# One decoder layer with a mixture of experts: the up layer's bias moved from a TensorE product to a VectorE add

## The chip, the cores and the metric

The kernel runs on one core of a Trainium2 chip. The metric is device time in microseconds (us) of the whole program, the median of several runs. A profiled execution has a time of its own; its span runs from the first to the last instruction.

## The reference

One post-norm decoder layer over 2048 tokens of width 256, in float32: self-attention, a cross-attention that reduces to two weight products, and a feed-forward part with 8 experts of which each token uses two, beside a shared expert.

```python
x = layernorm(x + self_attention(x))
x = layernorm(x + cross_attention(x, context))
scores = softmax(x @ gate_w.T); topk_w, topk_i = top_k(scores, 2)          # weights rescaled to sum to 1
h  = silu(einsum('nd,edh->neh', x, up_w) + up_b)                           # up_b: one row of 256 per expert
ye = einsum('neh,ehd->ned', h, down_w) + down_b
x = layernorm(x + einsum('ned,ne->nd', ye, comb) + shared_expert(x))
```

## The kernel before

All products run in TensorE with both operands split in two float32r parts (`hi` and the rest `lo`); `three` (L307) issues hi x hi, hi x lo and lo x hi. Engines are programmed one by one and meet at semaphores; the order on each engine is written out by hand.

*Before the loop.* Attention runs in 34 slots (`all_slots`, L338). The gate's choice gives each token two places in `xg_dram`, a buffer sorted by expert, and GpSimd scatters the rows there (`send`, L597). VectorE makes lists of tiles of 128 rows: `list_early` (L1712) those of tiles 0 to 16, in slot 33, and `list_later` (L1741) the other 22, inside the loop. `list_e` holds each tile's expert (8 for a tile that isn't used), `list_row` its first row. `rows` (128 x 10 x 256) holds the bias rows of all experts, split, on a few partitions; `sel` is a matrix of ones and zeros that adds those partitions up, so that the product of `sel` and one expert's rows puts a bias on all 128 partitions.

*The expert loop.* TILES = 39 tiles, on each engine one loop over i:

- TensorE (L1090): `tile_up(i)` (the bias product L1028, then six products in `three`), `tile_turn_x(i + 2)` (two transposes, L1018), `tile_turn_h(i - 1)` (L1042), `tile_down(i - 2)` (bias product L1050, six products). At i in LOADS (0, 4, 8, 12, 16, 17, 21, ...) it first loads up to four expert numbers from `list_e` into registers (L1096), and the weights are addressed by these. `PIECES_AT` adds products of the shared expert after turns 8 and 10.
- ScalarE (L1397): `tile_silu(i)` (L1319), `tile_x_hi(i + 2)` (L1312), `tile_h_hi(i - 1)` (L1325), `tile_y(i - 2)` (L1332). After turn 8 it takes an exponential (L1336) for the gate's weights, which changes its table, and silu changes it back.
- VectorE (L1975): `tile_x_lo(i + 2)` (L1829), a share of the small work (`drip`: one or two operations of `list_later`, `weigh`, later `add_experts(0)`), `tile_h_lo(i - 1)` (L1834), more small work. From turn 36 on the small work is `add_experts(0)`, which begins with a wait for rows fetched by SyncE.
- SyncE (L438): the load of tile i (L452) once the x rest of tile i - 4 is done. Then it waits until the results of tiles 0 to 30 have landed, fetches the expert rows of the first three quarters of the tokens (`load_y`, L454, L457), and those of the last quarter after tile 38.
- GpSimd (L710): `target_of(i + 8)` (L627), which needs the load of tile i + 8, then `send_y(i)` (L633), which scatters tile i's result to `y_dram`.

A turn is one value of i. The x rest and the h rest are what L1829 and L1834 write. Two tiles are in flight in `t_up` (PSUM) and `th` (SBUF), by i % 2.

*After the loop* VectorE adds the two weighted expert rows of each token (L1885), takes moments (L1895) and the last norm; TensorE does so for one quarter of the tokens and half of another (L1113).

## Time and profile before

| | before |
|---|---|
| median of 3 runs, us (lowest, highest) | 461.9 (460.45, 462.31) |
| the profiled execution, us | 463.2 |
| its span, us | 461.5 |
| mean granted TensorE clock, share of full | 0.987 |
| busy: TensorE, VectorE, ScalarE, GpSimd, us | 439.5, 309.3, 297.4, 211.4 |

Views of the profile are used as follows. The chain that ended last follows the last instruction back to what released it, step by step; its shares say which engine sets the time. The windows give each engine's busy time in a stretch. The timeline lists instructions by start. Busy time of an engine that others wait for counts; that of one that waits for others doesn't. TensorE's products overlap: their pace is the distance between starts, not their length.

### The profile page before, as it was taken

What the parts mean: (1) busy time and instruction counts of PE and PEld (TensorE: products, weight loads), DVE (VectorE), ACT (ScalarE), POOL (GpSimd) and SP (SyncE); (2) the same over time, 40 slices, a digit from 0 to 9 for tenths busy, and PEclk for the clock granted to TensorE, in tenths of its full rate; (3) what the DMA queues carried; (4) which work ended last, traced back from release to release, by engine and by line L of the source; (5) the groups of instructions that cost most, each with busy time, mean ns of one, the idle gap of its engine ahead of it and who ended that gap; (6) DMA issues with size and microseconds to landing.
All of it is one profiled execution on the core that took longest, in us unless ns stands there. A gap on an engine that the chain in (4) does not pass through costs nothing.

```text
span 461.5 us, 11060 instructions
## 1 busy us (share of the span) xinstructions
PE 439.5 (95%) x3657; PEld 396.7 (86%) x3657; DVE 309.3 (67%) x1249; ACT 297.4 (64%) x922; POOL 211.4 (46%) x246
## 2 busy tenths in 40 slices
PE   7999999999999999999999999989988999999991
PEld 6889898988989889898898998978778999999971
DVE  4366676878786757598676869698886734333495
ACT  3688656676666865668667567765523686776535
POOL 1899498440205011211166454473344686566521
PEclk9999999999999999999999999998998999999997
DMA  5950121400300000020021223021023654443576
GB/s 155 313 187 0 62 92 47 139 0 1 132 8 1 1 24 24 25 70 0 1 60 53 78 76 104 1 71 48 23 69 95 178 176 130 127 125 118 192 267 205
DMA packets 26543, 40.16 MB, mean 87 GB/s; under 512 B 3199, under 2 KB 17683, under 8 KB 26483
## 3 DMA queue, kind: packets, MB, share of 16 engines
q1 hardware_dynamic: 21532, 27.86, 19.7%
q0 software_dynamic: 3408, 9.33, 5.6%
q10 hardware_dynamic: 1547, 2.27, 1.6%
q8 instruction: 31, 0.51, 0.5%
q14 instruction: 25, 0.20, 0.2%
HBM read 26.83 MB, written 12.61 MB: 85 GB/s over the span
## 4 chain that ended last, share of the span: by engine, by line
PE 79%; DVE 9%; DMA 3%; issue 3%; ACT 2%; POOL 2%; SPq 1%; ACTq 0%; POOLq 0%; DVEq 0%
PE bank L309 17%; PE bank L310 17%; PE bank L311 17%; PE bank L825 7%; PE bank L836 7%; PE bank L875 6%; DMA w_raw<-y_dram 2%; PE bank L1018 2%; PE bank L776 1%; PE bank L920 1%; PE bank L1042 1%; POOL y_dram L633 1%; DMA xacc<-in_x_t 1%; DVE xacc L1885 1%; PE bank L1028 1%
## 5 line engine op out<-in xcount | busy, mean ns | idle before, releaser
L1201 ACT ACTIVATE probs<-probs,negmax 128x128 f32<-128x128 f32 x256 | 99.7, 393 | 26.5 <-DVE negmax L1470 26.5
L1470 DVE CUSTOM_DVE_ANT_0 probs<-bank,mask 128x128 f32<-128x128 f32 x256 | 62.4, 285 | 46.2 <-PE bank L825 46.2
L309 PE MATMUL bank<-w_hi,ot_hi 128*128 (+1 forms) x284 | 81.4, 287 | 3.5 <-DVE ot_lo L1496 3.5
L310 PE MATMUL bank<-w_lo,ot_hi 128*128 (+1 forms) x284 | 81.1, 286 | 0.0
L311 PE MATMUL bank<-w_hi,ot_lo 128*128 (+1 forms) x284 | 80.9, 285 | 0.0
L309 PE MATMUL bank<-xt_hi,w_hi 128*128 128x512 f32 (+1 forms) x148 | 59.7, 403 | 0.7 <-DVE xt_lo L1439 0.4
L1481 DVE TENSOR_TENSOR probs<-probs,rsum 128x512 f32<-128x512 f32 x64 | 58.6, 916 | 2.2
L309 PEld LDWEIGHTS bank<-w_hi,ot_hi 128*128 128x128 f32 x284 | 54.9, 193 | 4.1 <-issue 4.1
L610 POOL DMA_INDIRECT xg_dram<-xacc,place x32 | 34.0, 1062 | 53.0 <-PE bank L836 29.6
L310 PE MATMUL bank<-xt_lo,w_hi 128*128 128x512 f32 (+1 forms) x148 | 57.6, 389 | 0.0
L311 PE MATMUL bank<-xt_hi,w_lo 128*128 128x512 f32 (+1 forms) x148 | 57.6, 389 | 0.0
L311 PEld LDWEIGHTS bank<-w_hi,ot_lo 128*128 128x128 f32 x284 | 54.9, 193 | 0.0
L310 PEld LDWEIGHTS bank<-w_lo,ot_hi 128*128 128x128 f32 x284 | 54.7, 192 | 0.0
L1213 ACT ACTIVATE ot_hi<-bank,cols 128x512 fp32r<-128x512 f32 x32 | 22.0, 686 | 49.8 <-PE bank L875 49.8
L1164 ACT ACTIVATE qkv<-bank,cols 128x512 f32<-128x512 f32 x64 | 43.8, 684 | 10.9 <-PE bank L311 10.7
L1201 ACT ACTIVATION_READ_ACCUMULATOR probs<-probs,negmax 128x1 f32 x256 | 48.7, 190 | 0.0
L1829 DVE TENSOR_TENSOR ot_lo<-bank,ot_hi 128x256 fp32r<-128x256 f32 x39 | 16.5, 424 | 46.5 <-ACT ot_hi L1312 46.3
L633 POOL DMA_INDIRECT y_dram<-qkv,w_raw x39 | 40.6, 1041 | 14.3 <-ACT qkv L1332 8.4
L309 PE MATMUL bank<-w_hi,xt_hi 128*128 128x256 f32 x160 | 46.8, 292 | 0.0
L310 PE MATMUL bank<-w_lo,xt_hi 128*128 128x256 f32 x160 | 44.8, 280 | 0.0
L311 PE MATMUL bank<-w_hi,xt_lo 128*128 128x256 f32 x160 | 44.8, 280 | 0.0
L825 PE MATMUL bank<-qkv 64*128 64x128 f32 x512 | 37.2, 285 | 0.0
(237 smaller groups left out, 1059.5 us busy)
## 6 DMA issues: line engine op xcount, KB each, us to landing
qkv<-xg_dram SPq DMA_DIRECT2D x39, 128.5 KB, 2.4
ex_raw<-in_w_experts SPq DMA_DIRECT2D x18, 256.0 KB, 2.7
w_raw<-in_w_quads SPq DMA_DIRECT2D x10, 256.0 KB, 4.6
xacc<-in_x SPq DMA_DIRECT2D x4, 512.0 KB, 4.3
ex_raw<-in_w_cross SPq DMA_DIRECT2D x4, 512.0 KB, 3.8
w_raw<-in_ctx_t_in ACTq DMA_DIRECT2D x4, 512.0 KB, 3.8
w_raw<-in_w_quads SPq DMA_DIRECT2D x3, 512.0 KB, 6.5
xacc<-in_x_t SPq DMA_DIRECT2D x3, 512.0 KB, 6.8
```

What stands on the lines that cost most here:

```text
L309: pe.matmul(o, a_hi, b_hi, start=first, stop=False)
L310: pe.matmul(o, a_hi, b_lo, start=False, stop=False)
L311: return pe.matmul(o, a_lo, b_hi, start=False, stop=last)
L610: pool.indirect_dma_start(xg_dram, bass.IndirectOffsetOnAxis(ap=place[:, g, i, j:j + 1], axis=0), xacc[:, g * GT + j, :], None).then_inc(s ...
L633: pool.indirect_dma_start(y_dram, bass.IndirectOffsetOnAxis(ap=target[:, i:i + 1], axis=0), yt[:, i % YR, :], None).then_inc(y_sent[i % YR ...
L825: mm = pe.matmul(sc_bank[h][:, slices(j, P)], qt[s.ub][rows_h, s.pp, slices(j, P)], kt[s.ub][rows_h, s.pp, slices(j, P)], start=True, stop ...
L836: mm = pe.transpose(tr_bank[h][:, slices(j, P)], probs[:, 1 - s.par, h, slices(j, P)], ident[:, :])
L875: mm = pe.matmul(pv_bank[slices(h, DH), slices(j, P)], vb[:, j, c:c + DH], probs_t[:, h, slices(j, P)], start=True, stop=True)
L1164: nc.scalar.activation(dst, pj_bank[f % 2][:, :], ACT.Identity, bias=cols[:, b:b + 1]).then_inc(qk_ready, 1)
L1201: nc.scalar.activation(tile, tile, ACT.Exp, scale=-1.0, bias=negmax[:, s.par, h, j:j + 1], accum_out=sums[:, s.par, h, j:j + 1]).then_inc( ...
L1470: nc.vector.tensor_tensor_reduce(probs[:, s.par, h, slices(j, P)], sc_bank[h][:, slices(j, P)], mask[:, :], -SCALE, 3.0e38, ALU.add, ALU.m ...
L1481: nc.vector.tensor_tensor(tile, tile, rsum[:, h, :].unsqueeze(2).to_broadcast([P, GT, P]), ALU.mult).then_inc(probs_ready, 1)
```

## The change

The up layer's bias is no longer a product. ScalarE issues a transfer, `load_up_bias`, after the last attention transposes, which copies the eight experts' bias rows from DRAM to all 128 partitions: `up_bias`, 8 KB a partition, in the room of `probs`. In each turn VectorE does `tile_bias(i)`: PSUM `t_up` plus the expert's row, addressed by a register, to `th`; `tile_silu(i)` then reads and writes `th`. VectorE loads the expert numbers itself (`load_numbers`, at the same i as TensorE) from `list_b`, a second list with the number limited to 7. On ScalarE `tile_x_hi(i + 2)` now comes ahead of `tile_silu(i)`. Buffers that lay in `probs` (two of `hid`, one of `yg`) move elsewhere.

```diff
--- before.py
+++ after.py
@@ -172,6 +172,7 @@
         target_f = late[:, 3 * D:3 * D + TILES]
         tile_base = late[:, 3 * D + TILES:3 * D + 2 * TILES]
         target = late[:, 3 * D + P:3 * D + P + TILES].bitcast(U32)
+        list_b = late[:, 3 * D + P + TILES:3 * D + P + 2 * TILES].bitcast(I32)
 
         off = 2 * GROUP
         xg = qkv[:, off:off + XR * XW].rearrange("p (b n) -> p b n", b=XR)
@@ -182,10 +183,10 @@
         scale_by = [[qkv[:, off:off + 2 * GROUP].rearrange("p (t c n) -> p t c n", t=GT, c=2)[:, t, c, :] for c in range(2)]
                     for t in range(GT)]
         scale_last = [[probs_t[:, t, slices(2 * c, P)] for c in range(2)] for t in range(2)]
-        hid = [qkv[:, 0:2 * GROUP].rearrange("p (m n) -> p m n", m=2), probs[:, 0, :, :], probs[:, 1, :, :],
-               qkv[:, 0:2 * GROUP].rearrange("p (m n) -> p m n", m=2)]
+        hid = [qkv[:, o:o + 2 * GROUP].rearrange("p (m n) -> p m n", m=2)
+               for o in (0, 5 * GROUP + P, 10 * GROUP, 0)]
+        up_bias = probs[:, :, :, :].rearrange("p a h n -> p (a h n)").rearrange("p (e n) -> p e n", e=NE)
         crossed = [vv[0][:, slices(half, 2), :] for half in range(2)]
-        held = probs[:, :, :, :].rearrange("p a h n -> p (a h n)")
         marks = staged[:, 2 * GROUP:4 * GROUP]
         mark, marked = [marks[:, slices(i, EARLY * NE)].rearrange("p (t e) -> p t e", e=NE) for i in range(2)]
         summed = marks[:, 2 * EARLY * NE:2 * EARLY * NE + NE * NE].rearrange("p (a e) -> p a e", e=NE)
@@ -196,7 +197,7 @@
         xg_hi, hd_hi = [ot_hi[:, a, :].rearrange("p (b k n) -> p b k n", b=2, k=KT) for a in range(2)]
         xg_lo, hd_lo = [ot_lo[:, a, :].rearrange("p (b k n) -> p b k n", b=2, k=KT) for a in range(2)]
         yg = [[r.rearrange("p (t n) -> p t n", t=GT) for r in pair] for pair in
-              ((staged[:, 0:2 * GROUP], staged[:, 2 * GROUP:4 * GROUP]), (held[:, 0:2 * GROUP], held[:, 2 * GROUP:4 * GROUP]),
+              ((staged[:, 0:2 * GROUP], staged[:, 2 * GROUP:4 * GROUP]), (xt_hi[:, 0, 0:2 * GROUP].bitcast(F32), xt_hi[:, 1, 0:2 * GROUP].bitcast(F32)),
                (old, ex_raw[:, :, :].rearrange("p a n -> p (a n)")), (qkv[:, 0:2 * GROUP], qkv[:, 2 * GROUP:4 * GROUP]))]
 
         xg_dram = nc.dram_tensor("xg_dram", (XG_ROWS, XW), F32).ap()
@@ -270,6 +271,7 @@
         padded, pads_ready, cols_turned, cols_taken = (sem("padded"), sem("pads_ready"), sem("cols_turned"),
                                                        sem("cols_taken"))
         bias_moved = sem("bias_moved")
+        in_up_bias, th_biased = sem("in_up_bias"), sem("th_biased")
         rows_zeroed, in_up_rows, in_rows, rows_ready = (sem("rows_zeroed"), sem("in_up_rows"), sem("in_rows"),
                                                         sem("rows_ready"))
         sel_col_ready, sel_ready = sem("sel_col_ready"), sem("sel_ready")
@@ -1025,12 +1027,10 @@
                 if i == 1:
                     pe.wait_ge(logits_taken, G)
                 o = t_up[i % 2][:, 0:D]
-                pe.matmul(o, sel[:, 0, :], rows[:, bass.ds(e, 1), :].rearrange("p e n -> p (e n)"),
-                          start=True, stop=False)
                 hi, lo = of_expert(w_hi, e, 0), of_expert(w_lo, e, 0)
                 for k in range(KT):
                     mm = three(pe, o, xg_hi[:, i % 2, k, :], xg_lo[:, i % 2, k, :], hi[:, slices(k, D)],
-                               lo[:, slices(k, D)], False, k == KT - 1)
+                               lo[:, slices(k, D)], k == 0, k == KT - 1)
                 mm.then_inc(t_up_done, 1)
 
             def tile_turn_h(i):
@@ -1240,6 +1240,11 @@
                 nc.scalar.activation(crossed[half], cross_bank[G - 1][half][:, :].rearrange("p (j n) -> p j n", j=2),
                                      ACT.Copy).then_inc(cross_taken, 1)
 
+            def load_up_bias():
+                act.wait_ge(transposed, 2 * SLOTS)
+                act.dma_start(up_bias, up_rows[0:2 * NE, :].rearrange("c p -> (c p)").partition_broadcast(P)
+                              ).then_inc(in_up_bias, 16)
+
             def load_ctx(g):
                 if g == 0:
                     act.wait_ge(rows_ready, NX + 1)
@@ -1313,10 +1318,8 @@
                                      ACT.Copy).then_inc(xg_hi_ready, 1)
 
             def tile_silu(i):
-                act.wait_ge(t_up_done, i + 1)
-                if i >= 2:
-                    act.wait_ge(th_turned, i - 1)
-                nc.scalar.activation(th[:, i % 2, :], t_up[i % 2][:, 0:D], ACT.Silu).then_inc(th_ready, 1)
+                act.wait_ge(th_biased, i + 1)
+                nc.scalar.activation(th[:, i % 2, :], th[:, i % 2, :], ACT.Silu).then_inc(th_ready, 1)
 
             def tile_h_hi(i):
                 act.wait_ge(th_turned, i + 1)
@@ -1376,7 +1379,7 @@
                 soon.setdefault(after(g, 4), []).append(lambda g=g: take_x2(g, 0))
                 mid.setdefault(after(g, 4), []).append(lambda g=g: take_x2(g, 1))
             soon.setdefault(SLOTS - 1, []).append(lambda: take_cross(1))
-            behind[SLOTS] = [lambda: weights_exp(slice(0, TOK // P - GT)),
+            behind[SLOTS] = [load_up_bias, lambda: weights_exp(slice(0, TOK // P - GT)),
                              lambda: nc.scalar.activation(warm[:, :], warm[:, :], ACT.Silu)]
             all_slots(slot, behind)
             shared_hidden(0)
@@ -1395,10 +1398,10 @@
             for n in range(4):
                 more.setdefault(EARLY + 2 * GT + n, []).append(lambda n=n: make_scale_last(n))
             for i in range(TILES + 2):
+                if i + 2 < TILES:
+                    tile_x_hi(i + 2)
                 if i < TILES:
                     tile_silu(i)
-                if i + 2 < TILES:
-                    tile_x_hi(i + 2)
                 if 0 <= i - 1 < TILES:
                     tile_h_hi(i - 1)
                 if i >= 2:
@@ -1693,6 +1696,7 @@
                 yield
                 dve.wait_ge(dve_step, at)
                 nc.vector.tensor_copy(list_e[:, here], tile_e[:, here])
+                nc.vector.tensor_scalar(list_b[:, here], tile_e[:, here], float(NE - 1), None, ALU.min)
                 nc.vector.scalar_tensor_tensor(out=tile_base[:, here], in0=tile_e[:, here], scalar=float(REGION),
                                                in1=tile_row[:, here], op0=ALU.mult, op1=ALU.add)
                 at = issue(nc.vector.tensor_reduce(target_f[:, here], marked[:, :, :], AX.X, ALU.add))
@@ -1776,6 +1780,7 @@
                 yield
                 dve.wait_ge(dve_step, at)
                 nc.vector.tensor_copy(list_e[:, here], tile_e[:, here])
+                nc.vector.tensor_scalar(list_b[:, here], tile_e[:, here], float(NE - 1), None, ALU.min)
                 nc.vector.tensor_scalar(target_f[:, here], target_f[:, here], start[:, 0:1], float(P), ALU.add, ALU.mult)
                 at = issue(nc.vector.scalar_tensor_tensor(out=tile_base[:, here], in0=tile_e[:, here],
                                                           scalar=float(REGION), in1=tile_row[:, here], op0=ALU.mult,
@@ -1823,6 +1828,25 @@
                     tile = xacc[:, g * GT + 2 * half:g * GT + 2 * half + 2, 0:D]
                     nc.vector.tensor_tensor(tile, sdn_bank[g][half][:, :].rearrange("p (j n) -> p j n", j=2), tile,
                                             ALU.add).then_inc(shared_added, 1)
+
+            of_bias = {}
+
+            def load_numbers(i):
+                several = slice(i, min([j for j in LOADS if j > i] + [TILES]))
+                _, numbers = nc.values_load_multi_w_load_instructions(
+                    list_b[0:1, several], engines=[mybir.EngineType.DVE], min_val=0, max_val=NE - 1,
+                    skip_runtime_bounds_check_because="the list is made of compares that count to at most NE, and a min")
+                of_bias.update(zip(range(several.start, several.stop), numbers))
+
+            def tile_bias(i, e):
+                dve.wait_ge(t_up_done, i + 1)
+                if i == 0:
+                    dve.wait_ge(in_up_bias, 16)
+                if i >= 2:
+                    dve.wait_ge(th_turned, i - 1)
+                nc.vector.tensor_tensor(th[:, i % 2, :], t_up[i % 2][:, 0:D],
+                                        up_bias[:, bass.ds(e, 1), :].rearrange("p e n -> p (e n)"), ALU.add
+                                        ).then_inc(th_biased, 1)
 
             def tile_x_lo(i):
                 dve.wait_ge(xg_hi_ready, i + 1)
@@ -1973,6 +1997,11 @@
             for n, i in enumerate(PIECES_AT):
                 more.setdefault(i + 3, []).append(lambda n=n: last_hidden_lo(n))
             for i in range(TILES + 1):
+                if i in LOADS:
+                    dve.wait_ge(lists_ready, 1 if i < EARLY else 2)
+                    load_numbers(i)
+                if i < TILES:
+                    tile_bias(i, of_bias.pop(i))
                 if i + 2 < TILES:
                     tile_x_lo(i + 2)
                     if i == 0:
```

## Rows read from the trace of the kernel before

**Rows 1.** The page's chain that ended last: shares of the span by engine.

```profile
PE 79%; DVE 9%; DMA 3%; issue 3%; ACT 2%; POOL 2%; SPq 1%; ACTq 0%; POOLq 0%; DVEq 0%
```

**Rows 2.** Windows: us; busy PE, PEld, DVE, ACT, POOL; clock, DMA share, GB/s.

```profile
350.00:355.00 5.00, 5.00 (x58) 4.96 (x57) 3.00 (x13) 1.92 (x5) 1.32 (x2) 0.66 0.22 66
...
360.00:365.00 5.00, 4.96 (x42) 4.68 (x42) 4.86 (x20) 3.30 (x11) 2.16 (x3) 1.00 0.54 136
...
425.00:430.00 5.00, 5.00 (x45) 5.00 (x44) 1.51 (x4) 2.74 (x9) 3.64 (x6) 1.00 0.28 89
```

**Rows 3.** Timeline of TensorE, one quiet turn: start, length, instruction.

```profile
426.74 0.28 PE L1028 MATMUL bank<-rows,sel 128*128 x1
426.86 0.28 PE L309 MATMUL bank<-w_hi,ot_hi 128*128 x1
...
427.58 0.38 PE L1018 MATMUL bank<-ident,qkv 128*128 128x128 f32 x2
...
428.85 0.28 PE L1028 MATMUL bank<-rows,sel 128*128 x1
...
430.05 0.37 PE L1050 MATMUL bank<-rows,sel 128*128 x1
```

**Rows 4.** Timeline of ScalarE and VectorE, same turn; brackets: idle before, releaser.

```profile
427.78 0.38 ACT L1319 ACTIVATE qkv<-bank 128x256 f32<-128x256 f32 x1 [0.46 <-PE bank L311]
428.06 0.38 ACT L1312 ACTIVATE ot_hi<-bank 128x256 fp32r<-128x256 f32 x1
428.32 0.39 ACT L1325 ACTIVATE ot_hi<-bank 128x256 fp32r<-128x256 f32 x1
...
428.47 0.42 DVE L1829 TENSOR_TENSOR ot_lo<-bank,ot_hi 128x256 fp32r<-128x256 f32 x1 [1.36 <-ACT ot_hi L1312]
428.81 0.41 DVE L1834 TENSOR_TENSOR ot_lo<-bank,ot_hi 128x256 fp32r<-128x256 f32 x1
```

**Rows 5.** Groups by line in the loop: busy us, mean ns of one.

```profile
L1829 DVE TENSOR_TENSOR ot_lo<-bank,ot_hi 128x256 fp32r<-128x256 f32 x39 | 16.5, 424 | 46.5 <-ACT ot_hi L1312 46.3
...
L1305 ACT ACTIVATE xt_hi<-qkv 128x256 fp32r<-128x256 f32 x4 | 1.4, 410 | 0.0
```

**Rows 6.** Timeline of VectorE: the x rests that open turns 3 to 7.

```profile
358.26 0.42 DVE L1829 TENSOR_TENSOR ot_lo<-bank,ot_hi 128x256 fp32r<-128x256 f32 x1 [0.72 <-ACT ot_hi L1312]
...
360.60 0.42 DVE L1829 TENSOR_TENSOR ot_lo<-bank,ot_hi 128x256 fp32r<-128x256 f32 x1
...
362.92 0.41 DVE L1829 TENSOR_TENSOR ot_lo<-bank,ot_hi 128x256 fp32r<-128x256 f32 x1
...
364.95 0.41 DVE L1829 TENSOR_TENSOR ot_lo<-bank,ot_hi 128x256 fp32r<-128x256 f32 x1
...
366.99 0.42 DVE L1829 TENSOR_TENSOR ot_lo<-bank,ot_hi 128x256 fp32r<-128x256 f32 x1 [0.82 <-ACT ot_hi L1312]
```

**Rows 7.** Lines L1096 and L448 in queues: min/median/max ns, first and last start.

```profile
L1096 PEldq TENSOR_LOAD <-list_e x11: 318/534/1438, 348.7 to 431.9; - x11
...
L448 SPq FUSED_REGOPS  x39: 152/152/181, 342.7 to 423.0; - x39
```

**Rows 8.** Timeline of ScalarE: ahead of the loop, and the second table.

```profile
322.65 0.69 ACT L1213 ACTIVATE ot_hi<-bank,cols 128x512 fp32r<-128x512 f32 x1 [0.64 <-PE bank L875]
...
371.63 1.28 ACT L1319 ACT_TABLE_LOAD   x1
```

**Rows 9.** Timeline of SyncE's queue, GpSimd and VectorE towards the end.

```profile
424.47 0.34 SPq L452 DMA_DIRECT2D qkv<-xg_dram  x1
...
427.27 1.04 POOL L633 DMA_INDIRECT y_dram<-qkv,w_raw  x1 [0.33 <-POOL w_raw L627]
...
431.80 0.93 SPq L457 DMA_DIRECT2D w_raw<-y_dram  x2
...
436.41 0.88 DVE L1885 SCALAR_TENSOR_TENSOR xacc<-w_raw,xacc 128x256 f32<-128x256 f32 x2 [1.17 <-DMA w_raw<-y_dram]
...
443.42 1.67 DVE L1885 SCALAR_TENSOR_TENSOR xacc<-w_raw,xacc 128x256 f32<-128x256 f32 x4 [0.66 <-DMA w_raw<-y_dram]
```

## The prediction

> **What bounds the kernel now.** I read the chain of work that ended last first: 79% of the span is TensorE [rows 1]. The change sits in the expert loop, which runs from 349 to 440 us, so next come the windows of that stretch. In 425 to 430 us TensorE is busy all 5.00 us, VectorE 1.51 and ScalarE 2.74 [rows 2]: there TensorE alone sets the pace. In 360 to 365 us VectorE is busy 4.86 us and TensorE 4.96: two engines at their limit [rows 2]. In 350 to 355 us the granted clock averages 0.66, that is, part of it at 1.2 GHz [rows 2].
>
> One quiet turn shows the pace. The up products of tile 34 begin at 426.74 and those of tile 35 at 428.85, so a turn takes 2.11 us; the bias product occupies 0.12 of it, from 426.74 to 426.86 [rows 3]. In turn i TensorE does up(i), turns x of tile i+2, turns h of tile i-1 and does down(i-2). ScalarE then follows with silu at 427.78, the x copy at 428.06 and the h copy at 428.32; VectorE with the x rest at 428.47 and the h rest at 428.81, done at 429.22 [rows 4]. That h rest is needed by the down product at 430.05 [rows 3]: 0.83 us of slack.
>
> The end of the kernel does not hang on the loop's last tile. SyncE fetches the expert rows of three quarters of the tokens once the result of tile 30 has landed: issues from 431.80. VectorE waits for these rows until 443.42, after 0.66 us idle, and is then busy to the end [rows 9]. Tile 30's result is sent at 427.27, in GpSimd's queue behind work that needs the load of tile 38, issued at 424.47 [rows 9]; that load waits for the x rest of tile 34, which belongs to turn 32. So the savings of turns 0 to 32 reach the end, and those of 33 to 38 only help the last tiles.
>
> **The change, part by part.** *Removed:* 39 bias products on TensorE. For the end 33 count: 33 x 0.12 = 3.96 us. Two of them lie where the clock is at 1.2 GHz [rows 2] and take twice as long, about 0.1 more each; together 4.1 us.
>
> *Added on VectorE:* one add of 128x256 per tile, PSUM and SBUF in, SBUF out. The x rest has this shape and these memories: 424 ns [rows 5]; one behind another they start 0.34 apart (428.47 and 428.81, [rows 4]). In the quiet turn the add starts where silu did, 427.78, and is done at 428.20. The x copy on ScalarE, now first, needs the turned x (427.58 and 0.38, so 427.96, [rows 3]): 428.00 to 428.38. Silu follows at 428.28 and the h copy at about 428.60, since silu now reads SBUF (a ScalarE op of this size that does so takes 410 ns, [rows 5], against 0.38 us from PSUM, [rows 4]). The x rest then runs 428.42 to 428.84, the h rest 429.00 to 429.43. TensorE, 0.12 faster, wants it at 429.93: 0.5 us of slack remain, and silu, done at 428.69, has over 1 us. The add costs nothing there; without that cover every turn would pay it, 0.42 us.
>
> *The crowded turns.* From turn 3 on VectorE works through the second tile list beside its rests. It begins turns 3, 4, 5 and 6 at 358.26, 360.60, 362.92 and 364.95 [rows 6]: 2.34, 2.32 and 2.03 us without a pause, and 1.22 in turn 6, where the next rest at 366.99 follows 0.82 us idle [rows 6]. Each gains 0.34; turn 4 also gains the copy that makes the list for VectorE (0.1, small like its neighbours) and the loading of four expert numbers into registers. TensorE's own such load takes 534 ns at the median, 318 to 1438 at the ends [rows 7]; a register sum in front of a transfer takes 152 ns on SyncE's queue [rows 7]. I take 0.45 for the load, since the step waits among these small operations keep VectorE's queue from running ahead, and nothing for the register sums, which can run while the engine works. The four turns then ask 2.68 + 3.21 + 2.37 + 1.56 = 9.8 us of VectorE where TensorE asks 4 x 2.0 = 8.0. Of the 1.8 us excess the slack takes 0.5. So 1.3 us is lost: all that turns 0 to 8 had saved (9 x 0.12 and the 0.2 at the slow clock). Ends: 0, if VectorE enters with more in hand (it idled 0.72 before 358.26, [rows 6]); 2.3, if the load takes 1.44.
>
 No row here shows a register load on VectorE.
>
> *The table step.* After turn 8 ScalarE changes tables twice; the second load starts at 371.63 for silu(9) [rows 8]. The x copy that now stands ahead of silu must wait for the turned x, so silu and the h copy come about 0.3 us later and the x rest about 1.3 us earlier. The down product waits instead of the turning of x: I charge 0.2, ends -0.3 and 0.5.
>
> *Early and late.* The other list copy, in the first list, lies in VectorE's chain before the loop: 0.1. The table's transfer is issued by ScalarE where it had 0.64 us to spare before 322.65 [rows 8]; two such issues took 0.93 us on SyncE's queue [rows 9], so about 0.5 each. It is wanted some 25 us later: 0. Moving hidden and yg to other buffers adds no wait: 0. In turn 37 VectorE waits for the first expert rows (1.17 us before 436.41, [rows 9]), and bias(38), the h rest of tile 37 and, through silu, the last down products now queue behind it: the add's 0.34, less what TensorE is then ahead, makes the last result leave about 0.2 later against that transfer. What follows (the last quarter's rows) I charge 0, ends 0 and 0.6, because the three-quarter rows end later on VectorE.
>
> **Sum.** -4.1 + 1.3 + 0.2 + 0.1 = -2.5 us. The profiled execution took 463.2 (span 461.5 and 1.7 around it), 1.3 over the median of the runs, 461.9: 460.7 by the first, 459.4 by the second, which I predict. With all ends together the forecast spans -4.1 + 0 - 0.3 + 0.1 = -4.3 to -4.1 + 2.3 + 0.5 + 0.1 + 0.6 = -0.6: 457.6 to 461.3.
>
> **The rivals.** *A: the crowded turns cost nothing*, since drips slip into idle time behind them. For it: VectorE is idle 1.36 us a turn later [rows 4]; against it: 4.86 of 5 us busy [rows 2]. Gain 3.8 and more: 457.9.
>
> *B: the gain does not reach the end.* The chain there runs over GpSimd, a load, a landing and a transfer, where one late landing outweighs 20 turns of 0.12. Nothing says it must be late again. No gain, 0.3 of added work: 462.2.
>
> *C: TensorE's clock.* Waits of 0.2 to 0.4 us in each crowded turn, and about 2 us of idle TensorE before the last two down products, could bring spells at 1.2 GHz. In 350 to 355 us one followed the gaps ahead of the loop: at 0.66 of full clock [rows 2] 5 us did 3.3 us of full-clock work, 1.7 lost. Two such spells: +3.4, hence 462.8. Against it: in 360 to 365 us TensorE paused too, and the row reads 1.00 [rows 2].
>
> The Trainium skill, same page, section "HAM oscillation — how this bites in real kernels", says that idle gaps between bursts of products bring the slow clock back again and again; by that rule C happens in each turn with a gap, while the trace agrees for the long gaps ahead of the loop only.
>
> *D: slower.* The add with its register address sits in the path up, add, x rest, h rest, down in every turn. If it comes later by more than the 0.5 us of slack plus the 0.12 saved, the turn grows: the deciding point is 0.62 us of extra delay beyond the 0.42 of the add. A register sum of 0.15 and a load of 0.53 [rows 7], were they in every turn's path together with a wait that holds the queue, give 0.7: 0.08 x 39 = 3.1 us slower and 0.3 of the rest: 465.3. Against it: the load comes every fourth turn and finds 1.36 us of idle time.
>
> **How the numbers follow.** Runs of this kernel differ by about 0.5%, 2.3 us, which is what a measurement can tell from no change. Forecast 0.53 (0.33 beyond 0.5% faster, 0.20 within), A 0.12, B 0.11, C 0.08, D 0.16. Faster 0.33 + 0.12 = 0.45; same 0.20 + 0.11 + 0.08 = 0.39; slower 0.16. The range takes in the forecast, A, B and C, with a little more above for C: 457.6 to 463.2.
>
> **What would show it.** Turns of 2.0 us with VectorE about 2.5 busy in 5 us late in the loop; TensorE waiting for the h rest (or x rest) in turns 4 to 7, level with before at turn 8; a register load of about 0.5 us on VectorE's queue; SyncE's row fetch about 2.5 us earlier. Wrong if a quiet turn stays at 2.1 us, if the clock falls inside the loop, or if the fetch moves and the end does not.

## The result: slower by 1.4%, and what of it is the change

| | before | after |
|---|---|---|
| median of runs taken side by side, us (lowest, highest) | 462.1 (460.45, 463.17) | 468.7 (466.44, 469.69) |
| ratio, 95% interval | | 1.0139 [1.0094, 1.0183] |
| the profiled execution: span, us; mean granted clock | 461.5; 0.987 | 467.0; 0.975 |
| busy: TensorE, VectorE, ScalarE, GpSimd, us | 439.5, 309.3, 297.4, 211.4 | 440.9, 325.8, 300.4, 211.5 |

The forecast was 459.4 us, with a range to 463.2: wrong in sign. A second series of the same changed kernel (10 runs) gave a ratio of 1.006 [1.0018, 1.0102]. The two series differ by the clock that TensorE was granted: a mean of 0.978 in the first, 0.984 in the second. Windows of the profile of after, then of the same kernel in the second series (columns as in [rows 2], the clock third from the right):

```profile
345.00:350.00 5.00, 5.00 (x24) 5.00 (x25) 1.21 (x13) 0.00 (x0) 1.15 (x4) 0.50 0.19 55
350.00:355.00 5.00, 3.82 (x46) 2.96 (x45) 3.01 (x9) 0.77 (x2) 0.28 (x1) 0.50 0.20 53
...
365.00:370.00 5.00, 3.71 (x29) 3.09 (x28) 4.89 (x20) 2.55 (x8) 3.41 (x5) 1.00 0.66 180
...
430.00:435.00 5.00, 4.62 (x39) 4.55 (x39) 2.79 (x7) 3.21 (x10) 3.91 (x6) 1.00 0.30 98
```

```profile
345.00:350.00 5.00, 3.98 (x32) 3.77 (x32) 1.88 (x17) 0.38 (x1) 1.14 (x4) 0.94 0.30 82
350.00:355.00 5.00, 4.60 (x54) 4.31 (x54) 3.85 (x15) 1.40 (x5) 0.54 (x2) 0.74 0.21 54
```

Ahead of the loop TensorE runs at 1.2 GHz for a while in some executions and not in others: the profiles of e1, e4, e7 and e10 show 1.00 from 320 us into the loop, those of after and e13 0.50 from 342.5 to 357.5, that of before 0.66 [rows 2]. The spell is not the change's own, since e2, which has no add, shows 0.50 from 345 to 355. Whether the change makes it more frequent is not shown: the mean clock is 0.982 over its 14 runs and 0.985 over 113 of before. The first tile's result is copied out (ScalarE, L1335) at 360.14 us in this profile of after and at 357.67 in the other, at 356.74 in before and at 353.86 in experiment e10, whose code is that of after up to the first add: 3.4 of the 5.5 us by which the span of after is longer lie ahead of that copy.

Among the runs of one kernel the span falls by 3.0 us for each 0.01 of mean clock. Below, "at equal clock" is the mean span brought to a clock of 0.985 with that slope, less that of the 113 runs of before (461.7 us); two standard errors are 0.35 to 0.6 us (1.0 for e11), and against the runs of before of the same series alone no entry moves by more than 0.3. The ratios compare each kernel's fast runs alone; the figures at equal clock take all its runs, and by the fast ones alone they move by 0.3 us at most. So read, the changed kernel is 2.3 us slower (4 runs) and 2.2 (10 runs): that is what the change costs, 0.5%, as long as the clock itself is none of its doing, and what the experiments explain.

The chain that ended last names VectorE more than before [rows 1]:

```profile
PE 77%; DVE 14%; ACT 3%; issue 3%; DMA 2%; DVEq 0%; POOL 0%; ACTq 0%; SPq 0%; POOLq 0%
```

**A quiet turn** went as forecast. The timeline of after (start, length, instruction), to hold against [rows 3, 4]:

```profile
432.75 0.39 ACT L1335 ACTIVATE qkv<-bank 128x256 f32<-128x256 f32 x1
...
433.62 0.36 PE L1050 MATMUL bank<-rows,sel 128*128 x1
...
434.74 0.38 ACT L1335 ACTIVATE qkv<-bank 128x256 f32<-128x256 f32 x1
434.76 0.42 DVE L1858 TENSOR_TENSOR ot_lo<-bank,ot_hi 128x256 fp32r<-128x256 f32 x1 [0.23 <-ACT ot_hi L1328]
...
435.61 0.36 PE L1050 MATMUL bank<-rows,sel 128*128 x1
```

From copy to copy it takes 1.99 us, 2.11 before; the h rest is done at 435.18, 0.43 ahead of the down product. All turns below are read from these copies: "turn i" ends with the copy of tile i's result. The kernel's turn i does the down product of tile i - 2, so a register load of its turn 4, say, lengthens what is called turn 2 here.

**The opening** lost far more than forecast. VectorE ahead of the add of tile 4, then TensorE's waits for VectorE (a releaser "issue" is idle time in which the engine waited for nothing that the profile shows):

```profile
363.83 0.17 DVE L1774 TENSOR_SCALAR w_raw<-tile_e 128x22 f32<-128x22 f32 x1
364.64 0.42 DVE L1847 TENSOR_TENSOR qkv<-bank,probs 128x256 f32<-128x256 f32 x1 [0.64 <-issue]
```

```profile
365.55 0.41 PE L1020 MATMUL bank<-ident,qkv 128*128 128x128 f32 x2 [0.41 <-DVE ot_lo L1853]
366.39 0.41 PE L1042 MATMUL bank<-ident,qkv 128*128 128x128 f32 x2 [0.44 <-DVE ot_lo L1858]
369.12 0.41 PE L1042 MATMUL bank<-ident,qkv 128*128 128x128 f32 x2 [0.45 <-DVE ot_lo L1858]
371.62 0.41 PE L1042 MATMUL bank<-ident,qkv 128*128 128x128 f32 x2 [0.33 <-DVE ot_lo L1858]
```

Tiles 0 to 6 take 15.5 us, 12.9 before. The register loads themselves stand in the engine's queue (DVEq is VectorE's, PEldq TensorE's); the line gives ns min/median/max of one, and the start. VectorE's at 363.4 and in a quiet turn, and all of them:

```profile
L1836 DVEq TENSOR_LOAD <-w_raw x1: 1017/1017/1017, 363.4 to 363.4; - x1
...
L1836 DVEq TENSOR_LOAD <-w_raw x1: 353/353/353, 412.9 to 412.9; - x1
...
L1836 DVEq TENSOR_LOAD <-w_raw x11: 308/586/1401, 352.8 to 438.8; - x11
```

VectorE's loads take 1.0 to 1.4 us in the opening (ahead of the adds of tiles 0, 4, 8 and 12; 0.96 to 1.66 in the second profile) and 0.31 to 0.59 later. The one at 363.4 lasts until 364.42: one small operation ran beside it, and then VectorE stood idle.

**The load turns** of TensorE (loads ahead of the up products of tiles 21, 25, 29 and 33, seen in the copies of tiles 19, 23, 27 and 31) take 2.58 to 2.70 us; before they took 2.16 to 2.48. TensorE's own load, in before and in after:

```profile
L1096 PEldq TENSOR_LOAD <-list_e x1: 1003/1003/1003, 397.5 to 397.5; - x1
```

```profile
L1096 PEldq TENSOR_LOAD <-list_e x1: 1003/1003/1003, 403.5 to 403.5; - x1
```

What stands around it, before and after:

```profile
396.55 0.41 DVE L1834 TENSOR_TENSOR ot_lo<-bank,ot_hi 128x256 fp32r<-128x256 f32 x1
397.78 0.37 PE L1050 MATMUL bank<-rows,sel 128*128 x1
398.70 0.33 PE L1028 MATMUL bank<-rows,sel 128*128 x1
```

```profile
402.31 0.42 DVE L1858 TENSOR_TENSOR ot_lo<-bank,ot_hi 128x256 fp32r<-128x256 f32 x1 [0.23 <-ACT ot_hi L1328]
403.17 0.36 PE L1050 MATMUL bank<-rows,sel 128*128 x1
404.63 0.38 PE L311 MATMUL bank<-w_hi,ot_hi 128*128 x1 [0.39 <-issue]
```

Before, the h rest ends at 396.96, the load runs from 397.5 to 398.5, and the next turn's first product starts at 398.70, on time. After, the h rest ends at 402.73, the load runs from 403.5 to 404.5, and the product that was due at 404.24 starts at 404.63. The 0.83 us by which the h rest was early had not been idle time: one turn in four TensorE's queue used it to load registers.

### The profile page after: what moved, and what is told of

It reads as the page before. It is cut to its first block, busy times and chain, and to the rows that moved or that the text cites. A ratio compares the mean times of both kernels' runs of the same rounds, so it can differ in the third digit from the quotient of the medians.

```text
span 467.0 us, 11075 instructions
## 1 busy us (share of the span) xinstructions
PE 440.9 (94%) x3618; PEld 396.0 (85%) x3618; DVE 325.8 (70%) x1290; ACT 300.4 (64%) x922; POOL 211.5 (45%) x246
## 4 chain that ended last, share of the span: by engine, by line
PE 77%; DVE 14%; ACT 3%; issue 3%; DMA 2%; DVEq 0%; POOL 0%; ACTq 0%; SPq 0%; POOLq 0%
PE bank L311 17%; PE bank L312 16%; PE bank L313 16%; PE bank L827 7%; PE bank L838 6%; PE bank L877 6%; PE bank L922 2%; DVE xacc L1909 2%; PE bank L1020 2%; PE bank L778 1%; PE bank L1042 1%; DVE ot_lo L1858 1%; DMA xacc<-in_x_t 1%; DVE qkv L1847 1%; DVE stats L1919 1%
## 5 line engine op out<-in xcount | busy, mean ns | idle before, releaser
L311 PE MATMUL bank<-w_hi,ot_hi 128*128 (+1 forms) x284 | 82.9, 292 | 5.7 <-DVE ot_lo L1499 3.7
L1484 DVE TENSOR_TENSOR probs<-probs,rsum 128x512 f32<-128x512 f32 x64 | 56.5, 883 | 2.2
L311 PE MATMUL bank<-w_hi,xt_hi 128*128 128x256 f32 x160 | 47.8, 298 | 0.0
L312 PE MATMUL bank<-w_lo,xt_hi 128*128 128x256 f32 x160 | 45.8, 286 | 0.0
L313 PE MATMUL bank<-w_hi,xt_lo 128*128 128x256 f32 x160 | 45.8, 286 | 0.0
L827 PEld LDWEIGHTS bank<-qkv 64*128 64x128 f32 x512 | 31.1, 187 | 5.6 <-issue 4.3
```

The lines of the kernel that those rows point to most:

```text
L311: pe.matmul(o, a_hi, b_hi, start=first, stop=False)
L312: pe.matmul(o, a_hi, b_lo, start=False, stop=False)
L313: return pe.matmul(o, a_lo, b_hi, start=False, stop=last)
L827: mm = pe.matmul(sc_bank[h][:, slices(j, P)], qt[s.ub][rows_h, s.pp, slices(j, P)], kt[s.ub][rows_h, s.pp, slices(j, P)], start=True, stop ...
L1484: nc.vector.tensor_tensor(tile, tile, rsum[:, h, :].unsqueeze(2).to_broadcast([P, GT, P]), ALU.mult).then_inc(probs_ready, 1)
```

## The experiments

Theory after these readings: the change loses (1) in the opening, where VectorE sets the pace, by its adds and its register loads, and (2) in the load turns, where TensorE's own load has lost its cover. The main rival for (2): VectorE's load, issued in the same turns, delays the add. Stretches are between copies of the tiles named.

| kernel | ratio [95%] | at equal clock, us | tiles 0-15 | 15-34 | 34-38 |
|---|---|---|---|---|---|
| before | | 0 | 35.82 | 40.72 | 6.66 |
| after (second series) | 1.0060 [1.0018, 1.0102] | +2.2 | 38.43 | 40.40 | 7.36 |
| e1 | 1.0056 [1.0010, 1.0102] | +1.2 | 38.85 | 38.50 | 7.14 |
| e2 | 0.9949 [0.9915, 0.9983] | -2.1 | 34.78 | 39.30 | 6.28 |
| e3 | 1.0031 [1.0000, 1.0061] | 0.0 | 36.68 | 40.09 | 7.49 |
| e4 | 0.9990 [0.9945, 1.0036] | -0.9 | 35.87 | 40.16 | 6.16 |
| e5 | 0.9998 [0.9959, 1.0038] | -0.9 | 37.23 | 38.45 | 7.02 |
| e6 | 1.0001 [0.9958, 1.0043] | -0.4 | 37.10 | 38.89 | 6.52 |
| e7 | 1.0028 [0.9981, 1.0075] | 0.0 | 37.02 | 40.19 | 6.69 |
| e8 | 1.0007 [0.9959, 1.0055] | -0.7 | 37.11 | 38.82 | 6.46 |
| e9 | 0.9985 [0.9946, 1.0024] | -0.8 | 36.50 | 38.74 | 7.18 |
| e10 | 1.0089 [1.0042, 1.0136] | +2.3 | 38.77 | 40.18 | 7.36 |
| e11 | 1.0241 [1.0159, 1.0323] | +9.8 | 43.37 | 42.48 | 7.69 |
| e12 | 1.0000 [0.9964, 1.0035] | -0.9 | 36.50 | 39.23 | 6.15 |
| e13 | 1.0122 [1.0076, 1.0168] | +2.4 | 37.93 | 40.77 | 6.17 |
| e14 | 1.0071 [1.0037, 1.0104] | -0.1 | 35.33 | 39.20 | 6.09 |

**after_again**: the changed kernel, as it is.

> The changed kernel once more, for a second profile. In its first profile the clock is at 1.2 GHz from 341.6 to 358.4 us (granted 0.58 in 340 to 350), and the first result of the loop is 3.4 us later than in the kernel before. If such spells fall where they will, whatever the kernel, this profile has shorter ones or others, the first result of the loop comes within 1 us of the kernel before, and the end is 2 to 4 us earlier than in the first profile. If the change brings the spell, the granted clock in 340 to 350 us is again near 0.6 and the first result again some 3 us late. Time 466.5 to 469.7 either way.

The spell is shorter (0.94 in 345 to 350 us, where the first profile has 0.50), the first result comes 0.9 us after that of before, and the end 2.5 us earlier than in the first profile: the spell falls where it will. The median, 465.6, lies under the expected 466.5 to 469.7.

**e1_pe_load_early**: TensorE's loads one turn earlier, between the transposes of h and the down product.

```diff
                     tile_turn_h(i - 1)
+                if i + 1 in LOADS:
+                    load_experts(i + 1)
```

> The changed kernel with one edit: TensorE loads its expert numbers one turn earlier, between the turning of h and the down product, that is ahead of the wait for the h rest. Theory 1 (TensorE's own register load lost its cover, since its queue now gets past the wait for the h rest only 0.5 us ahead of the products instead of 0.83): the gaps of about 0.4 us ahead of the up products in the turns with a load go away, eight of them with 3.8 us in all; 3 to 3.5 us faster than the changed kernel, about 465. Rival (VectorE's register load delays the bias and with it everything behind): the turns with a load stay 0.4 us longer, time within 0.5 us of the changed kernel, 468.5.

The load turns fall to 1.99 us, with 2.06 to 2.26 in the turns before them, though VectorE's loads stay where they were: (2) holds, and its rival is not the main cause. The gain was put too high: 1.0 us at equal clock in place of 3 to 3.5. Tiles 15 to 34 gain 1.9, but the opening, where the loads moved too, takes 38.85 in place of 38.2 to 38.4.

**e2_no_product**: the kernel before without its bias product; the bias is left out.

```diff
-                pe.matmul(o, sel[:, 0, :], rows[:, bass.ds(e, 1), :].rearrange("p e n -> p (e n)"),
-                          start=True, stop=False)
```

> The kernel before with the 39 bias products of the up layer taken out and nothing in their place (the up layer's bias is left out). It measures what TensorE alone can give. Theory: 33 products of 0.12 us count for the end, with 0.2 more at the slow clock: 4.1 us faster than before, 458. Rival (the end does not follow the loop): within 1 us of before, 461 to 462.

All that the product is worth is 2.1 us at equal clock, not 4.1: its load turns take 2.26 to 2.52 with no add anywhere. So part of the lost cover comes with the product's removal alone.

**e3_fixed_rows**: after without VectorE's register loads; each tile gets the bias row of a fixed expert.

```diff
-                    load_numbers(i)
...
-                    tile_bias(i, of_bias.pop(i))
+                    tile_bias(i, i % NE)
```

> The changed kernel without VectorE's register loads: each tile takes the bias row of a fixed expert (i modulo 8), so VectorE's add has a constant address. The bias of the wrong expert is added. Theory 1 (TensorE's register load is what costs): the gaps ahead of the up products in the turns with a load stay near 0.4 us; only the crowded turn 4 gains some 0.6 us: 467.5 to 468. Rival (VectorE's register load costs): the gaps go, 3 us or more faster than the changed kernel, 465 or less.

VectorE's loads cost 2.2 us at equal clock, where 0.7 to 1.2 was expected, 1.5 to 1.75 of it in tiles 0 to 15. The load turns stay at 2.49 to 2.61, again TensorE's own load. What the four load turns take over quiet ones is 0.6 us in all in before, 1.45 in e2, 2.25 here and 2.6 in after: of the 2.0 that after loses there, 0.85 come with the product's removal, 0.8 with the add and 0.35 with VectorE's loads. With e2 the +2.2 of the change can be split at equal clock: product -2.1, adds and their waits +2.1 (e3 less e2), VectorE's loads +2.2 (after less e3). These are differences along one chain of kernels: they add up by construction, and in another order they may come out otherwise.

**e4_before_pe_early**: e1's edit on the kernel before, for the loads from turn 17 on.

> The kernel before (product kept, no add), with TensorE's register loads for the turns from 17 on moved one turn earlier, between the transposes of h and the down product. If those loads are hidden in the kernel before by the product and by the lead of TensorE's queue, as the theory has it, little is left to gain: turns 18 to 34 take 34.4 us before (16 turns at 2.11 and 0.6 over), so at most 0.6 us, ratio 0.998 to 1.000. If the early place costs as much there as the old place (the rival: a register load of TensorE costs its half microsecond wherever it stands), turns 18 to 34 take 34.4 us or more and the ratio is 1.000 or above.

Every turn from 18 to 34 takes 2.11 or 2.12, and from the copy of tile 18 to that of 34 it is 33.8 us: 0.6 gained, as the theory has it. In before, the load was nearly covered, and a little more lead covers it whole.

**e5_add_alone**: e3 and e4's edit together; the bias rows are e3's.

> The changed kernel without VectorE's register loads (each tile takes the row of a fixed expert number, so the bias is another expert's) and with TensorE's register loads from turn 17 on moved one turn earlier: what is left of the change is the add alone. Theory (TensorE's own load lost its cover, VectorE is the bound in the crowded opening turns): the load turns fall to 1.99 us each, the loop from the first tile's output copy to the last is 84.3 less 4 x 0.57 = 82.0 us against 83.2 before, the first six turns stay at 14.1, ratio about 0.997. Rival (TensorE's load costs 0.1 to 0.3 us in its new place too, as the turn before it took 2.06 to 2.26 in the first run of that edit): 82.7 us, and those turns stay over 1.99 although VectorE loads nothing.

The loop takes 82.70 us: the rival's number. The turns ahead of the loads take 2.21, 2.20, 2.01 and 2.16 with no load on VectorE: with the add in the chain, TensorE's load is not free at this place either.

**e7_thin_drips** (and the second and third edits of e6): VectorE's other work thinned.

```diff
-            more = {4: [lambda: last_x2_lo(0)], 5: [lambda: last_x2_lo(1)]}
+            more = {6: [lambda: last_x2_lo(0)], 7: [lambda: last_x2_lo(1)]}
...
                     tile_h_lo(i - 1)
-                    drip(parts, 2)
+                    drip(parts, 1)
```

> The changed kernel with VectorE's other work of the opening turns thinned alone: two small steps a turn in place of three, the two rests of the shared layer's last group in turns 6 and 7 in place of 4 and 5; its register loads and TensorE's stay where the change has them. Theory (VectorE's work is the bound there): the first six turns fall from 15.5 to 15.9 us to about 14, the later ones stay, ratio about 1.003 to 1.006 by what the other turns still lose. Rival 1 (VectorE's register load at turn 4 is the whole of the loss there): 15.5 us or more, nothing gained. Rival 2 (the steps that were moved only come later): turns 6 to 12 lose what the first six gain.

The first six turns take 14.02. Turns 3 and 4 fall from 2.72 and 2.50 to 2.02 and 2.11; turn 2, with a register load, falls from 3.41 to 2.88, and turn 6, with another, stays at 2.83. Some of the gain returns: turn 15 takes 2.82 in place of 2.30. VectorE's work is the bound there, as the prediction had it, only larger: at equal clock thinning takes off 2.2 us, as much as taking out VectorE's loads (e3).

**e6_mended**: e4's and e7's edits, and VectorE's loads `(0, 8)` in place of `(0, 4, 8, 12, 16)` for the first list.

> The changed kernel with three mends: TensorE's register loads from turn 17 on one turn earlier; VectorE's opening loads in two instructions, at turns 0 and 8, in place of five; the small steps of the tile list and the weights dripped two to a turn in place of three, and the two rests of the shared layer's last group in turns 6 and 7 in place of 4 and 5. Theory (in the crowded turns VectorE's work and its load are the bound): the first six turns fall from 15.5 to 15.9 us to about 13.3, the load turns to 2.0, the loop is about 82 us against 83.2 before, ratio about 0.996. Rival (the crowded turns are long because the add is one more step in the chain from product to Silu, whatever else VectorE does): the first six turns stay over 15 us, ratio 1.000 to 1.005.

The first six turns take 14.29, not 13.3. Turn 2, now without a load, takes 2.01, but turn 6 takes 3.96: the load of nine numbers ahead of add 8 lasts 2.5 us. Its line, and the add behind it:

```profile
L1843 DVEq TENSOR_LOAD <-w_raw x1: 2534/2534/2534, 368.7 to 368.7; - x1
```

```profile
371.50 0.42 DVE L1854 TENSOR_TENSOR qkv<-bank,probs 128x256 f32<-128x256 f32 x1 [1.67 <-issue]
```

**e10_load_behind_add** and **e8_mended_again**: VectorE's loads right behind the add of the turn before, alone and with the other mends.

```diff
                     tile_bias(i, of_bias.pop(i))
+                if i + 1 in LOADS:
+                    load_numbers(i + 1)
```

> The changed kernel with VectorE's register loads alone moved: right behind the add of the turn before, ahead of the x rest, and the first one ahead of the loop. TensorE's loads and the small steps stay where the change has them. Theory (place in the chain): turns 0 to 15 take 36.7 us, as without any load of VectorE, in place of 38.2 to 38.4; the later load turns stay at 2.55 to 2.65, since TensorE's own load makes them; ratio 1.003. Rival (full price at any place): 38 us and more, ratio 1.006.

> The changed kernel with TensorE's register loads from turn 17 on one turn earlier, VectorE's thinned opening (two small steps a turn, the shared layer's rests in turns 6 and 7) and VectorE's register loads, four numbers each as the change has them, moved from ahead of an add to right behind the add of the turn before, ahead of the x rest; the first one stands ahead of the loop. Theory (a load at the head of a turn delays add, Silu and h copy in a row; behind the add it lies in the time of Silu and h copy): turns 2 and 6, at 2.9 and 2.8 us with the thinned opening alone, fall to about 2.1, the turns ahead of the later loads from 2.2 to at most 2.1; the loop from the first output copy to the last takes 81.3 us against 83.2 before, ratio 0.996. Rival (VectorE's queue pays for a load in full wherever it stands): turns 2 and 6 stay at 2.8, loop 82.5 us, ratio 1.000.

The rival holds in both: e10 is no better than after, and in e8 turns 2 and 6 stay at 2.86 and 2.63. In the opening a load of VectorE is paid at both places tried, ahead of an add and behind one.

**e11_silu_first**: ScalarE's old order in the changed kernel.

> The changed kernel with ScalarE's old order, Silu ahead of the x copy. If the new order matters as the forecast of the quiet turn had it (the x copy runs during the add), the x copy now waits for the add and Silu: x rest and h rest come about 0.35 us later each, the quiet turn keeps under 0.2 us of slack, stays at 1.99, and turns with a register load or small steps grow by 0.2 to 0.4; ratio 1.010 to 1.02. Rival (the order is worth nothing, since ScalarE has the time): turns as in the changed kernel, ratio 1.006 to 1.014.

Worse than expected: 9.8 us over before at equal clock, 7.6 over the changed kernel, of which 5 in the opening; load turns take 2.9 to 3.35, quiet ones 1.99 to 2.08. The x copy ahead of Silu is what keeps the add cheap. Its profile is the only one with the clock under 1.00 between 362.5 and 380 us (0.71 in 367.5 to 370).

**e9_add_late_only** and **e12_add_middle**: adds for tiles 17 to 38, and 17 to 32; the product elsewhere.

```diff
-                               lo[:, slices(k, D)], False, k == KT - 1)
+                               lo[:, slices(k, D)], i in ADDED and k == 0, k == KT - 1)
```

> Tiles 0 to 16 take their bias from the product, as in the kernel before; tiles from 17 on from VectorE's add, with TensorE's register loads one turn earlier and VectorE's behind the add of the turn before. Theory (the change gains only in the quiet turns): turns up to 15 take 35.9 us as before (from the first output copy), the rest to the last 45.2 us (2.0 a turn) against 47.4 before; loop 81.1 against 83.2, ratio 0.9955. Rival (where the add starts is not what matters; the loop gives its gain back later in the wait for rows): the loop's end moves and the end of the kernel does not, ratio 1.000.

> VectorE's add for the tiles 17 to 32 alone, the product for the others; TensorE's register loads from turn 17 on one turn earlier. Theory (the change loses in the crowded opening and again in the last turns, where adds queue behind VectorE's waits for expert rows; it gains in the turns between): from the first output copy, turns to 15 take 35.9 to 36.5 us (before 35.8), 15 to 34 take 38.6 to 38.9 (before 40.7), 34 to 38 take 6.2 (6.2 with early loads alone, 7.2 with adds to the end), loop 81 us against 83.2; at equal clock 1.5 to 2 us faster than before, ratio 0.996. Rival (the last turns take longer because the loop comes to them earlier and waits there for something with its own time): 34 to 38 take 7 us or more, and the time stays 0.9 us under before, as with adds from 17 to the end.

Both expectations were too high: at equal clock they gain what e4 gains by its load alone. Tiles 15 to 34 gain 2.0 and 1.5 us on before, but tiles 0 to 15 lose 0.7: turn 7 takes 4.67, 4.05 before. There is no add in that turn, only ScalarE's new order at the table step. The 1.0 that e12 saves over e9 in tiles 34 to 38 does not show in its time.

**e13_no_late_adds**: after with the product kept from tile 33 on.

> The changed kernel with the product kept for the tiles from 33 on, all else as the change has it. Theory (adds behind the waits for expert rows): from the output copy of tile 34 to that of 38 takes 6.2 to 6.7 us in place of 7.4 to 7.7; opening and middle stay at 38.2 to 38.4 and 40.4. At equal clock it stays 1.5 to 2.2 us slower than before, since the end hangs on the expert rows fetched after tile 30 and these move little. Rival (an earlier loop waits there whatever does the adding): 7.4 or more.

Tiles 34 to 38 fall from 7.4 or 7.7 to 6.17, and the time stays, within 0.6 us (4 runs). The loss of the last turns is the adds', and taking them away gains nothing. The chain that ended last shows why. In both profiles of after its end runs over VectorE's last adds and h rests and no longer over the fetched expert rows; in e13 it runs over these rows, as it did in before. After, then e13:

```profile
440.00 0.43 DVE qkv L1847
...
443.48 0.42 DVE ot_lo L1858
443.90 0.79 DVE xacc L1909 x2
```

```profile
437.77 10.16 DMA w_raw<-y_dram
448.02 1.68 DVE xacc L1920 x4
```

Two paths end at nearly the same time there, and without the adds the other one sets the end.

**e14_all_mends**: adds for tiles 0 to 32, all of VectorE's numbers for the first list loaded ahead of the loop, with the mends of e4 and e7.

```diff
+            for n in LOADS:
+                if n < EARLY:
+                    load_numbers(n)
             for i in range(TILES + 1):
```

> The add for tiles 0 to 32 with every mend: VectorE's numbers for tiles 0 to 16 all loaded ahead of the loop, its opening thinned (two small steps a turn, the shared layer's rests in turns 6 and 7), TensorE's register loads from turn 17 on one turn earlier, the product kept from tile 33 on. Theory (a register load of VectorE costs about 0.8 us in a crowded turn and nothing ahead of the loop): turns 2 and 6 at 2.0 to 2.1, turns to 15 take 35.3 us (37.0 with the thinned opening alone), 15 to 34 take 38.9, 34 to 38 take 6.2, loop 80.4; at equal clock 2 to 2.5 us faster than before, ratio 0.995. Rival (turns 2 and 6 are long by something else that the add delays): they stay at 2.6 to 2.9, and the time ends at about that of the kernel before less 0.9.

The loop takes 80.62 us, turns 2 and 6 take 1.99 and 2.20, and nothing is won: the loads stand ahead of the first add now, and TensorE waits behind them. Tiles 0 to 15 take 35.33, 3.0 under after, about what e3 (1.6) and e7 (1.3) gain there together. Against it stand five loads in a row, of which the second to the fourth take 0.96 to 0.97 us each with VectorE idle:

```profile
L1853 DVEq TENSOR_LOAD <-w_raw x5: 310/964/1211, 352.2 to 356.4; - x5
```

```profile
356.98 0.42 DVE L1864 TENSOR_TENSOR qkv<-bank,probs 128x256 f32<-128x256 f32 x1 [3.31 <-issue]
...
357.88 0.41 PE L1021 MATMUL bank<-ident,qkv 128*128 128x128 f32 x2 [2.09 <-DVE ot_lo L1870]
```

Its runs had a mean clock of 0.976 (before 0.986 in the same series), hence the ratio. Here the clock may be the edit's own doing: behind TensorE's wait the profile shows 0.74 in 357.5 to 360 us and 0.58 in 360 to 362.5, where no other profile is under 1.00 in the second of these stretches. So the ratio, 0.7% slower, says more of e14 than the figure at equal clock. No version that adds the right bias beats the kernel before by more than its interval; e4, e9 and e12 are 0.8 to 0.9 us faster at equal clock (1.2, 0.6 and 0.7 against the runs of before of their own series).

## Why the prediction was wrong

By stretch, from the first copy on: the prediction's terms come to -0.3 us for tiles 0 to 15 (-1.8, +1.3, +0.2) and -2.3 for tiles 15 to 34 (19 x 0.12); after shows +2.35 to +2.6 and -0.3. So two steps failed: the load turns, by 2.0 us, and the opening, by 2.7 to 2.9.

**Removed: right for one turn, mis-sized in the sum.** 0.12 us a turn are saved where a quiet turn has no register load. The term of 4.1 us (its own parts add up to 4.2) measured 2.1 (e2): each load turn kept 0.3 to 0.5 us, and the opening gave 1.0 of 1.8.

**Added, quiet turns: the step that failed first.** "0.5 us of slack remain ... The add costs nothing there" is right for VectorE (0.43 measured) and wrong for TensorE. The slack of the h rest was taken from one turn without a load, as if nothing else used it. The rows held the warning: loads of up to 1438 ns [rows 7], of which the median of 534 hid two kinds of four numbers each, 0.33 to 0.53 in the opening and 1.0 to 1.44 later (the 534 itself is the last load, of two numbers). Four load turns take 0.6 to 0.7 over a quiet turn in the changed kernel, 0.5 more than before on average; moving the loads (e1) took 1.0 us off the time.

**The crowded turns: right place, mis-sized.** Forecast 1.3 us lost. Measured in tiles 0 to 15: 1.9 for the adds (e3 less e2; 0.5 of it in turn 7, the table step) and 1.5 to 1.75 for the loads (after less e3). The load of 0.45 us was taken near the middle of TensorE's; VectorE's took 1.0 to 1.4, at the end of the range. And it was charged once, for tile 4, while those of tiles 8 and 12 were charged nothing, as a load "finds 1.36 us of idle time"; turn 6, with the load for tile 8, took 2.75, 2.11 before.

By the Trainium skill, "TensorE: Matmul & The Clock Gate", section "Architectural detail: the array is 16× 32×32, not 1× 128×128", eight instructions can stand in VectorE's queue, in strict order. I had worked out 3.0 us of gain from that, the load running beside queued work; the page does not say that a load does so. The trace bears it out in part only: beside the load at 363.4 one operation ran, then VectorE stood idle for 0.64 us, and for 3.31 in e14.

**Table step** 0.2: turn 7 took 4.10 and 4.09 in the two profiles of after, 4.05 before; but 4.33 to 4.67 in eight of the other kernels with ScalarE's new order, and never over 4.09 with the old one. So the term measured 0.05 to 0.6, and what decides it was not tried.

**The end**: that it hangs on the rows fetched after tile 30 is right for before, by its chain, and for e13. In after VectorE's last adds and h rests are the end of the chain, which the prediction charged with 0 to 0.6; e13 leaves room for no more. From the copy of tile 30 to the end it takes 37.0 us in before and 36.6 to 36.9 in after, and tile 30's copy comes 2.3 to 2.5 us later after the first tile's: hence the 2.2 at equal clock.

**The rivals.** A falls (crowded turns cost 3.4 and more). B falls: the loss reaches the end. C: the clock did decide how much the first series showed, but not by waits in the turns: TensorE waited 0.33 to 0.45 us in the opening's turns, and the granted clock is 1.00 from 360 us to the loop's end in both profiles of after; the spells lie ahead of the loop. The rule named with C, read there as holding in each turn with a gap, does not hold for gaps of this length; in e11, whose turns lost more, the clock did fall inside the loop. D had the sign and, in part, the cause (a register load on the path), but not its place: not 0.08 us in every turn, but 0.5 in every fourth, on the other engine's own load, and 0.6 to 0.9 where VectorE loads for tiles 4 and 8.

**The signs** named beforehand: quiet turns took 1.99 us with VectorE 2.79 busy in 5, as forecast; TensorE did wait in the opening. But at the copy of tile 8 it was 2.5 us behind before, not level, and the row fetch came 4.0 us later (1.7 in the second profile), not 2.5 earlier.

## What to carry to other kernels

Before an engine's slack is spent, look what the *waiting* engine's queue does in it: a register load there is hidden only by the time between the last wait and the next product. Look at each kind of such an instruction in its own stretch, not at a median over all. And an operation moved to another engine takes its address registers with it: here, in an opening full of small work, VectorE's loads alone cost as much as the product was worth.

## What the runs showed of the hardware

A load of four numbers into registers took 0.34 to 0.59 us on VectorE in quiet turns and 0.96 to 1.66 in the opening; on TensorE 0.33 to 0.6 in the opening and 1.0 to 1.4 later; nine numbers on VectorE took 2.5, a single one took 0.31 on either engine in after. In the changed kernel it is long on the engine that sets the pace at the time, but work beside it is not the reason: in e14 it took 0.96 with VectorE idle. What decides it was not tried. The stretch at 1.2 GHz ahead of the loop came and went from run to run of one program, and with it up to 6 us of the span: over the runs of before the mean clock went from 0.970 to above 0.990, the span from 466 to 460.
